# Start and end of a modulated, routed feed-forward kernel: the first demodulation factors worked out for 16 batches alone, both halves of x scaled on VectorE for six groups, one set of positions behind a transposition, and the last block's sums finished one after the other

## The chip, the cores and the metric

The kernel runs on one core of a Trainium2 chip. The metric is the device time of one execution in microseconds (us); lower is better. A core has five engines with an instruction queue each: TensorE (PE in the profile, its weight loads apart as PEld), VectorE (DVE), ScalarE (ACT), GpSimd (POOL) and SyncE (SP). They wait for each other by semaphores.

## The reference

x is 128 batches of 64 tokens with 256 features (8192 tokens). Each batch has a condition vector y. A layer scales and projects the tokens, and a mixture of 8 experts with 2 chosen per token follows; its result is added to x.

```
ys = y * scale
d = rsqrt(einsum('bi,io->bo', ys*ys, weight*weight) + 1e-8)
hidden = einsum('bsi,io->bso', x * ys[:, None, :], weight) * d[:, None, :]
logits = hidden @ wr.T;  vals, idx = top_k(logits, 2)
gating = softmax over the two chosen
pos = cumsum(mask) - 1;  keep = mask & (pos < 2560)      # slot of a token in its expert
h = gelu(xg[e] @ w1[e] + b1[e]);  y = h @ w2[e] + b2[e]  # F = 1024
out = x + segment_sum(y * gate, token)
```

## The kernel before

**The front.** The 8192 tokens are worked on in 16 groups of 512 (8 batches each), four groups to a set. Features lie on partitions, in a lower and an upper half of 128. For each group g: x is scaled by ys (`scale_x`: the lower half in eight ScalarE instructions, one for each batch, L717; the upper half in one of VectorE, L856; for group 0 alone VectorE does the lower half too, L860). TensorE makes the two halves of the product in `modulate(g)` (L501; four matmuls, which the trace shows as eight records; three banks `m_bank` take turns, so half number c waits until half c-3 has been read). `scale_hidden(g)` multiplies them by d (lower half: eight ScalarE instructions, L752; upper half: one of VectorE, L912). `turn_back(g)` on TensorE turns the result back to rows of tokens, four tiles a group, with the router's logits (L514, L516); three banks take turns, so that the fourth tile waits for the copy of the first by ScalarE (`copy_back`, L737). On TensorE group g's `turn_back` stands behind `modulate(g+1)`. x has a ring of four tiles; SyncE loads group g+4 once `modulate(g)` is done.

d comes out of a product of the squares (L485, after 44 warm-up matmuls at L481): VectorE adds epsilon for all 128 batches (`var_t`, 256 columns, L862), ScalarE takes the root (L721), VectorE inverts it (L865) and refines it in four steps (L867 to L873).

For each set, VectorE's `choose` finds the two experts and writes `mask` (L934), TensorE's `positions` counts (L530 to L535), VectorE's `find_slots` and `set_gates` follow, and ScalarE takes one exponential (`odds`, L742). VectorE's `list_group` and TensorE's `list_slots` (L549) make the token lists of each expert. From group 2 on ScalarE also splits a piece of expert 0's weights a group (`split_piece`, L728), and VectorE subtracts (L881). Every engine runs its own list in program order.

**The blocks.** After the front, blocks of up to 384 slots (the last ones of an expert have 256) are gathered, go through `first_product` (L594 to L596), GELU on ScalarE twice (L784), a rounding remainder on VectorE (`split_chunk`, L1169), and `second_product` (L607 to L609, three matmuls for each slice s of 128 slots and each chunk f of eight). At the end of a block VectorE adds a bias (`add_bias`, L1191) and multiplies by the gate (`weigh`, L1197), and GpSimd adds the rows into the output by one indirect DMA for each slice (L425); where a block has two slices, one of 16 spare rows stands ahead of them (L418). In the last block the two slices' sums share one bank, and `y_done` is raised once for both.

## Time and profile before

| | |
|---|---|
| Time, median of 3 runs | 919.29 us (919.23 to 919.46) |
| The profiled execution: its own time, its span | 920.08 us, 918.1 us |
| PE busy, DVE busy, ACT busy, POOL busy | 98%, 53%, 60%, 48% of the span |
| Granted TensorE clock, mean | 0.996 |
| First matmul of group 0 / of block 0 (after the front) | at 8.66 us / at 110.94 us |
| Last matmul ends | near 906.75 us |

Times of the trace are microseconds from the start of the span. The span is what the instructions cover; the execution's own time lies about 2 us over it, and the median of the three unprofiled runs 0.8 us under that.

### The profile page before, as it was taken

To read this page: it belongs to the slowest core of one execution; us is meant where nothing else is said; L and a number is where in the kernel's file an instruction comes from. 1 tells how busy PE (TensorE), PEld (TensorE's weight loads), DVE (VectorE), ACT (ScalarE), POOL (GpSimd) and SP (SyncE) were. 2 spreads that over 40 slices of the span, in tenths; PEclk is the share of its full clock that TensorE was granted. 3 is DMA by queue.
4 is the path that set the end of the run, shared out by engine and by line. 5 is a ranking of instruction groups with operands and counts; after the bars stand their busy time and mean duration, and the time that the engine had idled before them with its cause. 6 is when DMAs were issued, how large, how long until landed. Compare 5 with 4: busy or idle time off the path is not lost.

```text
span 918.1 us, 20295 instructions
## 1 busy us (share of the span) xinstructions
PE 896.6 (98%) x6605; PEld 859.7 (94%) x6605; DVE 484.0 (53%) x1155; ACT 552.1 (60%) x1331; POOL 436.8 (48%) x473
## 2 busy tenths in 40 slices
PE   8999999999999999999999999999999999999995
PEld 5566799999999999999999999999999999999994
DVE  4498877536454554545444554445455544444442
ACT  5988655656556665666556665665566655655552
POOL 0000304645546645665446645655566534664543
PEclk9999999999999999999999999999999999999998
DMA  9676392442523442343523442345234322342232
GB/s 346 208 245 220 105 347 45 67 124 54 132 42 57 66 126 47 54 64 52 134 36 53 69 115 55 59 60 134 42 51 70 47 41 42 50 67 36 47 47 25
DMA packets 56142, 84.47 MB, mean 92 GB/s; under 512 B 6864, under 2 KB 45296, under 8 KB 55696
## 3 DMA queue, kind: packets, MB, share of 16 engines
q0 software_dynamic: 28624, 38.21, 26.9%
q1 hardware_dynamic: 25760, 44.87, 14.5%
q8 instruction: 37, 0.61, 0.3%
q10 hardware_dynamic: 1696, 0.58, 0.2%
q14 instruction: 25, 0.20, 0.1%
HBM read 53.71 MB, written 38.32 MB: 100 GB/s over the span
## 4 chain that ended last, share of the span: by engine, by line
PE 92%; DVE 4%; ACT 2%; issue 1%; DMA 1%; POOLq 0%; ACTq 0%; SPq 0%; DVEq 0%; POOL 0%
PE bank L594 14%; PE bank L607 14%; PE bank L596 14%; PE bank L608 14%; PE bank L609 14%; PE bank L595 14%; PE bank L582 3%; PE bank L501 3%; PE bank L514 1%; PE bank L516 1%; PE bank L549 1%; DMA sb_w<-in_w 1%; DVE sb_w_lo L881 0%; ACT sb_hid_t L752 0%; POOLq L94 0%
## 5 line engine op out<-in xcount | busy, mean ns | idle before, releaser
L784 ACT ACTIVATE sb_h_raw<-bank,sb_b_now 128x384 f32<-128x384 f32 (+1 forms) x416 | 223.6, 538 | 250.1 <-PE bank L596 235.0
L1169 DVE TENSOR_TENSOR sb_h_lo<-sb_h_raw,sb_h_hi 128x384 fp32r<-128x384 f32 (+1 forms) x416 | 213.8, 514 | 264.8 <-ACT sb_h_hi L784 240.3
L607 PE MATMUL bank<-sb_w_hi,sb_h_hi 128*128 128x256 f32 x1064 | 304.4, 286 | 0.0
L608 PE MATMUL bank<-sb_w_lo,sb_h_hi 128*128 128x256 f32 x1064 | 299.8, 282 | 0.0
L425 POOL DMA_INDIRECT out_rows<-sb_y,sb_add_ids x154 | 253.7, 1647 | 95.5 <-issue 55.5
L609 PE MATMUL bank<-sb_w_hi,sb_h_lo 128*128 128x256 f32 x1064 | 298.7, 281 | 0.0
L594 PE MATMUL bank<-sb_xt_hi,sb_w_hi 128*128 128x384 f32 (+1 forms) x832 | 264.1, 317 | 1.5 <-ACT sb_h_hi L784 1.4
L595 PE MATMUL bank<-sb_xt_lo,sb_w_hi 128*128 128x384 f32 (+1 forms) x832 | 260.2, 313 | 0.0
L596 PE MATMUL bank<-sb_xt_hi,sb_w_lo 128*128 128x384 f32 (+1 forms) x832 | 260.2, 313 | 0.0
L784 ACT ACTIVATE sb_h_hi<-bank,sb_b_now 128x384 fp32r<-128x384 f32 (+1 forms) x416 | 221.0, 531 | 0.0
L609 PEld LDWEIGHTS bank<-sb_w_hi,sb_h_lo 128*128 128x128 f32 x1064 | 200.8, 189 | 0.0
L608 PEld LDWEIGHTS bank<-sb_w_lo,sb_h_hi 128*128 128x128 f32 x1064 | 200.4, 188 | 0.0
L607 PEld LDWEIGHTS bank<-sb_w_hi,sb_h_hi 128*128 128x128 f32 x1064 | 200.3, 188 | 0.0
L404 POOL DMA_INDIRECT sb_xg<-hidden,sb_gather_ids x133 | 140.3, 1055 | 70.9 <-POOL sb_ids_ring L400 43.6
L594 PEld LDWEIGHTS bank<-sb_xt_hi,sb_w_hi 128*128 128x128 f32 x832 | 156.4, 188 | 3.0 <-ACT sb_h_hi L784 2.1
L595 PEld LDWEIGHTS bank<-sb_xt_lo,sb_w_hi 128*128 128x128 f32 x832 | 156.6, 188 | 0.0
L596 PEld LDWEIGHTS bank<-sb_xt_hi,sb_w_lo 128*128 128x128 f32 x832 | 156.5, 188 | 0.0
L397 POOL COPY sb_gather_ids<-sb_ids 128x3 int32 (+2 forms) x52 | 10.0, 192 | 300.2 <-DVE sb_gates L1163 172.1
L1154 DVE TENSOR_TENSOR sb_xt_lo<-bank,sb_xt_hi 128x384 fp32r<-128x384 f32 x104 | 53.2, 553 | 74.8 <-ACT sb_xt_hi L759 74.7
L759 ACT CAST sb_xt_hi<-bank 128x384 fp32r<-128x384 f32 x104 | 44.9, 484 | 77.8 <-PE bank L596 75.8
L1191 DVE TENSOR_TENSOR sb_y<-bank,sb_b 128x256 f32<-128x256 f32 x133 | 49.0, 419 | 52.2 <-PE bank L609 49.9
L501 PE MATMUL bank<-sb_x,sb_w 128*128 128x512 f32 x128 | 57.9, 595 | 0.9 <-ACT sb_hid_t L752 0.8
(144 smaller groups left out, 586.1 us busy)
## 6 DMA issues: line engine op xcount, KB each, us to landing
sb_w_raw<-in_w SPq DMA_DIRECT2D x16, 1024.0 KB
hidden<-sb_rows SPq DMA_DIRECT2D x4, 2112.0 KB, 10.0
sb_x<-in_x_t SPq DMA_DIRECT2D x16, 512.0 KB, 5.5
out_rows<-in_x SPq DMA_DIRECT2D x16, 512.0 KB, 7.5
out_rows<-sb_y,sb_add_ids POOLq DMA_INDIRECT x156
sb_xg<-hidden,sb_gather_ids POOLq DMA_INDIRECT x133
sb_b<-in_b SPq DMA_DIRECT2D x1, 1024.0 KB, 10.0
hidden<-sb_empty SPq DMA_DIRECT2D x4, 132.0 KB, 7.9
```

The costliest lines, as they stand in the source:

```text
L404: pool.indirect_dma_start(xg[:, s, :], None, hidden[0:PAD + sets * TS * P, :], bass.IndirectOffsetOnAxis(gather_ids[:, s:s + 1], axis=0),) ...
L425: pool.indirect_dma_start(out, bass.IndirectOffsetOnAxis(add_ids[:, s:s + 1], axis=0), y[s][:, :], None, compute_op=ALU.add,).then_inc(add ...
L501: mm = pe.matmul(m_bank[c % M_RING][:, :], w_sb[:, k, o * P:(o + 1) * P], x_in[g % X_RING][:, k, :], start=(k == 0), stop=(k == KC - 1))
L594: pe.matmul(h, w_hi[u][:, cols], xt_hi[:, rows], start=(k == 0), stop=False)
L595: pe.matmul(h, w_hi[u][:, cols], xt_lo[:, rows], start=False, stop=False)
L596: mm = pe.matmul(h, w_lo[u][:, cols], xt_hi[:, rows], start=False, stop=(k == KC - 1))
L607: pe.matmul(y, hi, w_hi[u][:, cols], start=(f == 0 and s != 1), stop=False, skip_group_check=True)
L608: pe.matmul(y, hi, w_lo[u][:, cols], start=False, stop=False, skip_group_check=True)
L609: mm = pe.matmul(y, lo, w_hi[u][:, cols], start=False, stop=(f == FC - 1), skip_group_check=True)
L784: ins = act.activation(h[:, 0:subs * P], h_bank[f % H_BANKS][:, 0:subs * P], ACT.Gelu_apprx_tanh, bias=b1_now[u][:, f:f + 1])
L1154: dve.tensor_tensor(xt_lo[:, rows_k], x_bank[k][:, 0:SLOTS], xt_hi[:, rows_k].bitcast(F32), ALU.subtract).then_inc(xt_ready, 1)
L1169: dve.tensor_tensor(h_lo[f % RING][:, cols], h_raw[f % RING][:, cols], h_hi[f % RING][:, cols].bitcast(F32), ALU.subtract).then_inc(h_read ...
```

## The change

Six edits. (1) d is worked out in two parts, `D_PARTS`: the 16 batches of groups 0 and 1 (32 columns), then the other 112 (224 columns). (2) VectorE scales the lower half of x too for groups 0 to 5 (`BOTH_HALVES = 6`, `scale_lower`), and ScalarE starts with group 6. (3) For set 0, TensorE's `positions(0)` stands behind `turn_back(4)` instead of ahead of it. (4) ScalarE's `odds` stands behind `copy_back`, for the first three sets. (5) In the last block of the last expert (`last_block`) the last four chunks of slice 0 are all added up ahead of those of slice 1, slice 1 has a bank of its own, the spare rows' DMA is left out, and the last DMAs have a semaphore of their own. (6) 66 warm-up matmuls instead of 44.

```diff
-WARM = 44
+WARM = 66
+BOTH_HALVES = 6
+FIRST_BATCHES = 2 * GB
+        D_PARTS = (slice(0, FIRST_BATCHES), slice(FIRST_BATCHES, B))
 # TensorE
             def modulate(g):
-                if g == 0:
-                    pe.wait_ge(xs_first, 1)
+                if g < BOTH_HALVES:
+                    pe.wait_ge(xs_first, g + 1)
                 else:
-                    pe.wait_ge(xs_lower, g)
+                    pe.wait_ge(xs_lower, g + 1 - BOTH_HALVES)
...
-                if g % JOINED == 1 and g > JOINED:
+                first_set = g == JOINED + 1
+                if g % JOINED == 1 and g > JOINED and not first_set:
                     positions(g // JOINED - 1)
                 turn_back(g - 1)
+                if first_set:
+                    positions(0)
...
+            def last_block(u, b):
...
+                    if f - 3 < FC - RING:
+                        chunk_split(b, f - 3)
+                        for s in range(SHORT):
+                            second_product(u, f - 3, SHORT, only=s)
+                for s in range(SHORT):
+                    for f in range(FC - RING, FC):
+                        chunk_split(b, f)
+                        second_product(u, f, SHORT, only=s)
 # ScalarE
-            act.wait_ge(set_dve, 5)
-            act.activation(root_t[:, :], var_t[:, :], ACT.Sqrt).then_inc(set_act, 1)
-            scale_x(1)
+            for i, part in enumerate(D_PARTS):
+                act.wait_ge(var_ready, i + 1)
+                act.activation(root_t[:, :, part], var_t[:, :, part], ACT.Sqrt).then_inc(set_act, 1)
...
-            act.wait_ge(set_dve, 10)
+            act.wait_ge(d_ready, 1)
             scale_hidden(0)
             for g in range(GROUPS):
-                if g + 2 < GROUPS:
+                if BOTH_HALVES <= g + 2 < GROUPS:
                     scale_x(g + 2)
                 if g + 1 < GROUPS:
                     scale_hidden(g + 1)
-                if g % JOINED == 0 and g > 0:
-                    odds(g // JOINED - 1)
                 if g == GROUPS - 1:
                     split_rows(0)
                 copy_back(g)
+                if g % JOINED == 0 and g > 0:
+                    odds(g // JOINED - 1)
 # VectorE
+            scale_x(0)
+            scale_lower(0)
+            dve.wait_ge(set_pe, 1)
+            for part in D_PARTS:
+                dve.tensor_scalar(var_t[:, :, part], var_bank[:, :, part], EPS, None, ALU.add).then_inc(var_ready, 1)
+            scale_x(1)
+            inverse(0)
+            factors(0)
+            scale_lower(1)
+            inverse(1)
+            scale_hidden(0)
+            factors(1)
...
             for g in range(GROUPS):
-                scale_hidden(g)
+                if g > 0:
+                    scale_hidden(g)
                 if g + 2 < GROUPS:
                     scale_x(g + 2)
+                if g + 2 < BOTH_HALVES:
+                    scale_lower(g + 2)
 # GpSimd
-                if subs < SUBS:
+                if subs < SUBS and not last:
```

On VectorE this is the stretch from the sum of squares to group 1's result, before the change (`sb_var_t`, `sb_root_t` and `sb_tmp_t` are steps of d; `sb_hid_t` is the product times d):

```order
L860 TENSOR_TENSOR sb_x<-sb_x,sb_ys_t 128x512
L862 TENSOR_SCALAR sb_var_t<-bank 128x256
L856 TENSOR_TENSOR sb_x<-sb_x,sb_ys_t 128x512
L865 RECIPROCAL sb_root_t<-sb_root_t 128x256
L867 TENSOR_TENSOR sb_tmp_t<-sb_root_t 128x256
L869 TENSOR_TENSOR sb_tmp_t<-sb_tmp_t,sb_var_t 128x256
L871 TENSOR_SCALAR sb_tmp_t<-sb_tmp_t 128x256
L873 TENSOR_TENSOR sb_d_t<-sb_tmp_t,sb_root_t 128x256
L875 CAST sb_tri<-sb_tri_f 128x128
L912 TENSOR_TENSOR sb_hid_t<-bank,sb_d_t 128x512
```

and after it, from the second half of the scaled x of group 1 on:

```order
L894 TENSOR_TENSOR sb_x<-sb_x,sb_ys_t 128x512
L917 RECIPROCAL sb_root_t<-sb_root_t 128x2x16
L924 TENSOR_TENSOR sb_tmp_t<-sb_root_t 128x2x16
L926 TENSOR_TENSOR sb_tmp_t<-sb_tmp_t,sb_var_t 128x2x16
L928 TENSOR_SCALAR sb_tmp_t<-sb_tmp_t 128x2x16
L930 TENSOR_TENSOR sb_d_t<-sb_tmp_t,sb_root_t 128x2x16
L900 TENSOR_TENSOR sb_x<-sb_x,sb_ys_t 128x512
L917 RECIPROCAL sb_root_t<-sb_root_t 128x2x112
L909 TENSOR_TENSOR sb_hid_t<-bank,sb_d_t 128x512
L924 TENSOR_TENSOR sb_tmp_t<-sb_root_t 128x2x112
```

The factors of 16 batches now come first and the other part's behind the lower half of x (L900), with group 0's upper half of the result between.

On ScalarE this is the stretch around the first set's exponential, before the change (from group 3's weight piece to the scaling of x for group 7):

```order
L728 CAST sb_w_hi<-sb_w_raw 128x512
L717 ACTIVATE sb_x<-sb_x,sb_ys_t 128x64 x8
L752 ACTIVATE sb_hid_t<-bank,sb_d_t 128x64 x8
L742 ACT_TABLE_LOAD
L742 ACTIVATE sb_ratio<-sb_gap 128x16
L737 COPY sb_rows<-bank 128x264 x4
L728 CAST sb_w_hi<-sb_w_raw 128x512
L717 ACTIVATE sb_x<-sb_x,sb_ys_t 128x64 x8
```

and after it:

```order
L766 CAST sb_w_hi<-sb_w_raw 128x512
L755 ACTIVATE sb_x<-sb_x,sb_ys_t 128x64 x8
L791 ACTIVATE sb_hid_t<-bank,sb_d_t 128x64 x8
L775 COPY sb_rows<-bank 128x264 x4
L780 ACT_TABLE_LOAD
L780 ACTIVATE sb_ratio<-sb_gap 128x16
L766 CAST sb_w_hi<-sb_w_raw 128x512
L755 ACTIVATE sb_x<-sb_x,sb_ys_t 128x64 x8
```

The table load and the exponential moved from ahead of the four copies of group 4 to behind them; the first L755 in this piece is the first that ScalarE has at all now.

## Rows read from the trace of the kernel before

**Rows 1.** The page: busy time of each engine, share of the span, instructions.
```profile
PE 896.6 (98%) x6605; PEld 859.7 (94%) x6605; DVE 484.0 (53%) x1155; ACT 552.1 (60%) x1331; POOL 436.8 (48%) x473
```

**Rows 2.** Windows: length, busy us (instructions) of PE, PEld, DVE, ACT, POOL; granted clock, DMA share, GB/s.
```profile
50.00:60.00 10.00, 9.89 (x52) 6.17 (x51) 10.00 (x17) 9.06 (x38) 0.00 (x0) 1.00 1.07 372
```

**Rows 3.** Timeline to 5.4 us, then to 15: start, length, engine, line, count, [idle<-releaser].
```profile
1.43 4.21 PE L481 MATMUL bank<-sb_ones 128*128 128x128 bf16 x38 [1.43 <-DVE sb_ones L838]
...
1.43 4.54 PE L481 MATMUL bank<-sb_ones 128*128 128x128 bf16 x44 [1.43 <-DVE sb_ones L838]
...
7.42 1.16 PE L485 MATMUL bank<-sb_ysq_t,sb_wsq 128*128 128x128 f32 x8 [1.44 <-DVE sb_wsq L850]
...
8.66 5.39 PE L501 MATMUL bank<-sb_x,sb_w 128*128 128x512 f32 x12
...
9.55 1.75 DVE L865 RECIPROCAL sb_root_t<-sb_root_t 128x256 f32<-128x256 f32 x1
...
13.04 1.75 ACT L752 ACTIVATE sb_hid_t<-bank,sb_d_t 128x64 f32<-128x64 f32 x8 [1.63 <-DVE sb_d_t L873]
...
14.84 1.98 PE L501 MATMUL bank<-sb_x,sb_w 128*128 128x512 f32 x4 [0.79 <-ACT sb_hid_t L752]
```

**Rows 4.** Timeline, groups 2 and 3: one scaling of x, TensorE's products.
```profile
17.47 0.68 DVE L856 TENSOR_TENSOR sb_x<-sb_x,sb_ys_t 128x512 f32<-128x512 f32 x1
...
19.21 3.60 PE L501 MATMUL bank<-sb_x,sb_w 128*128 128x512 f32 x8
...
24.49 3.60 PE L501 MATMUL bank<-sb_x,sb_w 128*128 128x512 f32 x8
```

**Rows 5.** Timeline, VectorE, two small instructions of the gates.
```profile
48.07 0.25 DVE L940 RECIPROCAL sb_gate<-sb_gate 128x16 f32<-128x16 f32 x1
...
48.36 0.17 DVE L941 TENSOR_TENSOR sb_gate<-sb_gate,sb_ratio 128x16 f32<-128x16 f32 x1
```

**Rows 6.** Timeline, TensorE and ScalarE, 35 to 50 us (groups 5 to 7).
```profile
35.30 3.60 PE L501 MATMUL bank<-sb_x,sb_w 128*128 128x512 f32 x8
...
35.78 0.62 ACT L728 CAST sb_w_hi<-sb_w_raw 128x512 fp32r<-128x512 f32 x1
...
39.96 1.28 ACT L742 ACT_TABLE_LOAD   x1
...
40.95 0.23 PE L530 MATMUL bank<-sb_mask,sb_tri 128*128 128x128 bf16 x1 [2.04 <-DVE sb_mask L934]
...
41.26 0.22 ACT L742 ACTIVATE sb_ratio<-sb_gap 128x16 f32<-128x16 f32 x1
...
43.48 3.60 PE L501 MATMUL bank<-sb_x,sb_w 128*128 128x512 f32 x8
...
43.96 0.62 ACT L728 CAST sb_w_hi<-sb_w_raw 128x512 fp32r<-128x512 f32 x1
...
47.98 0.97 ACT L737 COPY sb_rows<-bank 128x264 f32<-128x264 f32 x3
...
49.00 3.60 PE L501 MATMUL bank<-sb_x,sb_w 128*128 128x512 f32 x8
...
49.48 0.62 ACT L728 CAST sb_w_hi<-sb_w_raw 128x512 fp32r<-128x512 f32 x1
```

**Rows 7.** Timeline, 903 us to the last instruction.
```profile
903.71 0.28 PE L607 MATMUL bank<-sb_w_hi,sb_h_hi 128*128 128x256 f32 x1
...
904.78 0.42 DVE L1169 TENSOR_TENSOR sb_h_lo<-sb_h_raw,sb_h_hi 128x256 fp32r<-128x256 f32 x1 [1.00 <-ACT sb_h_hi L784]
...
906.79 0.42 DVE L1191 TENSOR_TENSOR sb_y<-bank,sb_b 128x256 f32<-128x256 f32 x1 [1.58 <-PE bank L609]
...
907.43 0.35 DVE L1197 TENSOR_SCALAR sb_y<-sb_y,sb_gates 128x256 f32<-128x256 f32 x1 [0.22 <-DVE sb_y L1191]
...
908.59 1.57 POOL L425 DMA_INDIRECT out_rows<-sb_y,sb_add_ids  x1 [1.13 <-DVE sb_y L1197]
...
910.46 1.55 POOL L425 DMA_INDIRECT out_rows<-sb_y,sb_add_ids  x1 [0.30 <-issue]
```

More of the change, by code:

```diff
@@ L387, in _ @@
             sp.wait_ge(plan_ready, 1)
-            n_all = all_blocks(sp)
-            sp.wait_ge(added, n_all * (16 * SUBS))
+            but_last = all_blocks(sp, less=1) + (LAG - 1)
+            sp.wait_ge(added, but_last * (16 * SUBS))
             sp.sem_inc(sp_paced)
+            sp.wait_ge(added_last, 16 * SHORT)
         @block.gpsimd
@@ L407, in gather, with adds @@
                     ).then_inc(gathered if s < SHORT else gathered_third, 16)
-            def adds(b, subs=SUBS):
+            def adds(b, subs=SUBS, last=False):
                 if not isinstance(b, int) or b > 0:
@@ L427, in adds @@
                         y[s][:, :], None, compute_op=ALU.add,
-                    ).then_inc(added, 16)
+                    ).then_inc(added_last if last else added, 16)
             def next_block(k, tile, sets=SETS, subs=SUBS):
@@ L473, in _ @@
             for i in range(LAG):
-                adds(rest + i, SHORT)
+                adds(rest + i, SHORT, last=(i == LAG - 1))
         @block.tensor
@@ L597, in first_product, with second_product @@
                 mm.then_inc(h_open, 1)
-            def second_product(u, f, subs=SUBS):
+            def second_product(u, f, subs=SUBS, only=None):
                 cols = slice(WCOLS + f * D, WCOLS + (f + 1) * D)
-                for s in range(subs):
+                for s in range(subs) if only is None else (only,):
                     hi = h_hi[f % RING][:, s * P:(s + 1) * P]
                     lo = h_lo[f % RING][:, s * P:(s + 1) * P]
-                    y = y_bank[s]
-                    pe.matmul(y, hi, w_hi[u][:, cols], start=(f == 0 and s != 1), stop=False, skip_group_check=True)
+                    y = y_bank[s] if only is None else last_y_bank[s]
+                    pe.matmul(y, hi, w_hi[u][:, cols], start=(f == 0 and (s != 1 or only is not None)), stop=False,
+                              skip_group_check=True)
                     pe.matmul(y, hi, w_lo[u][:, cols], start=False, stop=False, skip_group_check=True)
                     mm = pe.matmul(y, lo, w_hi[u][:, cols], start=False, stop=(f == FC - 1), skip_group_check=True)
-                    if f == FC - 1 and s > 0:
+                    if f == FC - 1 and only is not None:
+                        mm.then_inc(y_done, 1)
+                    elif f == FC - 1 and s > 0:
                         mm.then_inc(y_done, SUBS - subs + 1)
@@ L655, in one_block @@
                 second_product(u, FC - 1, subs)
+            def last_block(u, b):
+                bank_read(b, 0)
+                first_product(u, 2, SHORT)
+                for f in range(3, FC):
+                    bank_read(b, f - 2)
+                    first_product(u, f, SHORT)
+                    if f == 3:
+                        pe.wait_ge(y_read, b * SUBS + SUBS)
+                    if f - 3 < FC - RING:
[6 more added lines that the diff above has]
+                        second_product(u, f, SHORT, only=s)
             pe.wait_ge(gathered, 16 * SHORT)
@@ L682, in expert @@
                 if e == E - 1:
-                    one_block(u, None, end - 1, so_far, subs=SHORT)
+                    last_block(u, end - 1)
                 else:
@@ L856, in scale_x, with scale_lower, scale_hidden @@
                 dve.tensor_tensor(cols, cols, by_batch(ys_t, 1, g), ALU.mult).then_inc(xs_upper, 1)
+            def scale_lower(g):
+                dve.wait_ge(x_loaded[g % X_RING], 16 * (g // X_RING + 1))
+                cols = x_in[g % X_RING][:, 0, :].rearrange("p (b s) -> p b s", s=S)
+                dve.tensor_tensor(cols, cols, by_batch(ys_t, 0, g), ALU.mult).then_inc(xs_first, 1)
+            def scale_hidden(g):
+                dve.wait_ge(d_ready, 1 if g < 2 else 2)
+                if g >= 2:
+                    dve.wait_ge(back_done, TILES * (g - 1))
+                c = KC * g + 1
+                dve.wait_ge(m_done, c + 1)
+                dve.tensor_tensor(hid_t[g % 2][:, 1, :].rearrange("p (b s) -> p b s", s=S),
+                                  m_bank[c % M_RING][:, :].rearrange("p (b s) -> p b s", s=S),
+                                  by_batch(d_t, 1, g), ALU.mult).then_inc(hid_upper, 1)
@@ new lines, in inverse, with factors @@
+            def inverse(i):
+                part = D_PARTS[i]
+                dve.wait_ge(set_act, i + 1)
+                dve.reciprocal(root_t[:, :, part], root_t[:, :, part]).then_inc(d_step, 1)
+            def factors(i):
+                part = D_PARTS[i]
+                root, tmp = root_t[:, :, part], tmp_t[:, :, part]
+                dve.wait_ge(d_step, 4 * i + 1)
+                dve.tensor_tensor(tmp, root, root, ALU.mult).then_inc(d_step, 1)
+                dve.wait_ge(d_step, 4 * i + 2)
+                dve.tensor_tensor(tmp, tmp, var_t[:, :, part], ALU.mult).then_inc(d_step, 1)
+                dve.wait_ge(d_step, 4 * i + 3)
+                dve.tensor_scalar(tmp, tmp, -0.5, 1.5, ALU.mult, ALU.add).then_inc(d_step, 1)
+                dve.wait_ge(d_step, 4 * i + 4)
+                dve.tensor_tensor(d_t[:, :, part], tmp, root, ALU.mult).then_inc(d_ready, 1)
@@ L1220, in one_block @@
                 for s in range(subs):
-                    add_bias(e, b, s, subs)
+                    add_bias(e, b, s, subs, last)
                     if last:
```

43 lines of the change are left out of this document (14 added, 29 removed).

## The prediction

> **What bounds the kernel now.** The page first: TensorE is busy 98% of the span, no other engine over 60% [rows 1]. So a gain has to come from time in which TensorE stands still, and a loss from a new stand. I looked for its gaps in the timeline, engine by engine. They lie at the two ends: in the front (groups 0 to 15) and behind the last matmul. In the blocks between TensorE runs through, so a shift of the front reaches the end whole. Four stands matter here. Half 3 of the products starts at 14.84, after a stand of 0.79 for ScalarE's scaled result, which itself had waited 1.63 for d until 13.04 [rows 3]. Group 2 starts at 19.21 [rows 4], after a turn in which the fourth tile waited for the first one's copy. `positions(0)` at 40.95 waits 2.04 for the mask [rows 6]. And from the last matmul to the last indirect DMA it is a chain: bias, gate, then GpSimd's two DMAs of 1.57 and 1.55, the second right behind the first [rows 7].
>
> **Warm-up, 22 more matmuls.** 44 take 4.54 us, 0.103 each [rows 3], and end 1.44 before L485, which waits for VectorE. At that mean 22 more cost 2.27 and would end 0.8 late. But the mean hides two paces. The first 38 take 4.21, 0.11 each (128 columns at 1.2 GHz); the last six add 4.54 - 4.21 = 0.33, 0.055 each, the upper level [rows 3]. There 22 cost 1.2, less than the 1.44. I take 0; the other end is +0.8.
>
> **d for 16 batches, and x on VectorE.** Nothing in the trace has 32 columns. A reciprocal takes 0.25 at 16 columns [rows 5] and 1.75 at 256 [rows 3], 6.3 ns a column, so 0.35 at 32 and 1.55 at 224. A product takes 0.17 at 16 [rows 5]; I take 0.19, and 0.04 between dependent ones. The walk on VectorE: epsilon for the first part starts when L485 ends (7.42 + 1.16, so 8.6) and takes 0.2, for the second 0.4, with 0.08 overlap (to 9.1); upper half of x, group 1, 0.68 [rows 4] (to 9.7); reciprocal 0.35 (10.0); four small steps at 0.23 (10.95). ScalarE's `scale_hidden(0)` starts at about 10.97 instead of 13.04 and ends, 1.75 later, at 12.7. TensorE's first 12 records end the pipelined way at 8.66 + 5.39 - 0.16 = 13.9 (0.16 is how far a record reaches over the next start). Half 3 is then held by nothing: 13.9 instead of 14.84.
>
> VectorE pays for it: `scale_lower(1)` ends at 11.5, and TensorE wants it at 12.2 (slack 0.6). Then reciprocal 1.55, `scale_hidden(0)` 0.68 (as wide), four steps near 0.42, the cast 0.2, both halves of x of group 2 at 0.68: 16.95. TensorE's half 3 ends at 13.9 + 1.72 = 15.62, `turn_back(0)` takes 1.85 (5.28 from 19.21 to 24.49 [rows 4], less 3.44 for a group's products), so it wants group 2 at 17.47 (slack 0.5). ScalarE no longer has `scale_x` between, scales group 1 by 15.7 and copies tile by tile, so the fourth tile's stand goes as well. Group 2 starts at 17.47 instead of 19.21: **1.74 us**. For groups 2 to 5 ScalarE loses eight instructions each and VectorE gains one of 0.68; both stay under TensorE's 5.28 a group. The two groups from 24.49 to 35.30 take 10.81 where 2 x 5.28 is 10.56: **0.25 us**. Group 5 starts at 33.32. The loads of x are issued by the same counts, up to 2 us earlier; group 4's is wanted after 23 us and is priced at nothing.
>
> **Positions behind the turn, exponential behind the copies.** ScalarE's weight piece starts 0.48 behind group 5 (35.78 against 35.30), so at 33.80. From there to the mask's use is 5.17 (40.95), so `positions(0)` may start at 38.97; `turn_back(4)` now lies ahead of it and fills the 2.04 stand. From 40.95 to 43.48 is 2.53 with a turn of 1.85 in it: positions cost 0.68, and group 6 starts at 39.65, 3.8 earlier [rows 6]. That isn't kept, for ScalarE is late next. From 33.80 it needs 4.18 to where the table load stands now (39.96): 37.98. Four copies take 1.50 (47.98 to 49.48): 39.48. Table load 1.28 and exponential about 0.22, which used to lie in ScalarE's wait for TensorE, now stand on its path: 40.98. From its weight piece to the start of group 7 it was 43.96 to 49.00, 5.04, and group 7 starts at 46.02 instead of 49.00 [rows 6]. The gain is 2.98, so this part adds 2.98 - 1.99 = **0.99 us**. VectorE waits for the same weight piece and is then busy without a gap (10.00 of 10 us in 50 to 60 [rows 2]), so its lists come earlier by the same 3.0. For set 1 the exponential moves in the same way, without a table load, some 0.22 again [rows 6]: **-0.2 us**. Set 2's lies beside slack: 0.
>
> At that point a page of the Trainium skill speaks against the change. The row has 1.28 for the load, and the exponential starts at 41.26, 0.02 behind it [rows 6]. The Trainium skill, ScalarE: Activation LUTs, What ACT_TABLE_LOAD costs, adds a drain of about 1380 ns to the load's 1283 ns, some 2.66 us for a switch. The trace agrees with the load alone. By the page the sum below would be 1.4 smaller.
>
> **The last block.** Slice 0 has twelve matmuls from 903.71 on, at 0.12 (24 matmuls from 903.71 to 906.79, less one's 0.28, over 23). Nine end at 904.79; the last three need the remainder of chunk 7, ready at 904.78 + 0.42 and 0.06 for the signal, 905.26. So TensorE stands 0.47, and slice 0 is whole at 905.26 + 0.24 + 0.28, read at 905.83 instead of 906.79: 0.96. Slice 1 is whole at 907.22, goes through bias and gate (0.42 + 0.22 + 0.35) and the 0.81 that GpSimd takes to start: 909.07. GpSimd's first DMA starts at 907.63, its second at 910.46 - 0.96 = 909.50, behind the first and not behind slice 1 (slack 0.4). The spare rows' DMA would have ended just there; leaving it out is worth about 0.1 that is in this sum. **0.96 us**.
>
> **Sum.** 1.74 + 0.25 + 0.99 - 0.20 + 0.96 = 3.74. The profiled execution would go from 920.08 to 916.3 (span 914.4); the runs' median lies 0.8 under it, so 919.29 becomes **915.5**. A run of this kernel tells 0.2% (1.8 us) from nothing.
>
> **Rivals.**
> - *The small steps cost as much as the whole ones.* Upper ends: 1.75 and 0.46 a step. Then d comes at 13.3, `scale_lower(1)` at 13.9, TensorE waits 1.7 for group 1, and the first term is gone: 917.3. Against it, 16 columns take 0.25 and 0.17 [rows 5]. 0.05.
> - *The table switch costs 2.66 now that work stands right behind it.* 1.38 less: 916.9. Against it, the exponential runs 0.02 behind the load [rows 6]. 0.05. That is the price of the Trainium skill's page named above.
> - *ScalarE isn't the one that holds group 7* (copies overlap more). TensorE alone would start it at 39.65 + 5.28 = 44.9, gain 4.1: 914.5. 0.06.
> - *The front gives its gain back* between 50 and 100 us, where VectorE has no gap [rows 2]: one more 2 to 3 us in its list before the second mask, as a wait for ScalarE's weight pieces, and only the end's 0.96 stays: 918.3, no change. For it, both engines are nearly full there; against it, nothing is added there but 0.2. 0.08.
> - *Slower: TensorE's clock.* If the longer warm-up is followed by a fall to 1.2 GHz, each L501 record costs 0.43 more. 9 such records eat the forecast, 13 make it slower by over 0.2%; both of groups 0 and 1 (16 records) give +6.9, 922.4. Against it: in the trace the pace rises within the 44, and L501's records are at the upper level behind 1.44 of idleness, which now shrinks to 0.2 [rows 3]. 0.03.
>
> **How the numbers follow.** The forecast has 0.71, with 914.9 to 916.5 of its own (slacks of 0.4 to 0.6 at three places, warm-up +0.8). The range takes in the small steps and ScalarE's rival: 914.5 to 917.3. Faster by over 0.2%: 0.71 + 0.05 + 0.05 + 0.06 and 0.02 for what I didn't think of, 0.89. Within: 0.08. Slower: 0.03.
>
> **What would show it.** Right: half 3 of the products starts near 13.9 without a stand; group 2 at 17.5, group 5 at 33.3, group 7 at 46.0, with a stand in the turn before it; block 0's first matmul near 108.2 (now 110.94); the last two indirect DMAs start 1.87 apart, near 904.9 and 906.7. Wrong: TensorE waiting for `sb_x` in groups 1 to 5, a gap behind the table load, L501 records 0.86 apart, or a second DMA that starts later than 0.3 behind the first.

## The result: slower by 0.8%, and the profile after

The changed kernel takes 927.11 us (median of 6 runs, 926.68 to 930.26), the kernel before 919.46 in the same comparison; the ratio is 1.0082 (95% interval 1.0060 to 1.0103). The forecast was 915.5. The profiled execution of the changed kernel takes 929.16 us, its span is 927.0, 8.9 above before; that is 2.05 above the median of its own runs, so the trace shows somewhat more loss than the medians (7.65). Four executions in all the comparisons (one of the changed kernel with x's halves on VectorE for two groups, three of the kernel before) took 1094 us or more and are left out.

The page of the changed kernel: busy time, the queue that brings code (`q14 instruction`: packets, MB, share), and the chain that ended last. Behind it the same queue's line of the page of before.

```profile
PE 903.6 (97%) x6627; PEld 866.5 (93%) x6627; DVE 486.7 (52%) x1166; ACT 543.0 (59%) x1292; POOL 436.4 (47%) x472
...
q14 instruction: 34, 0.28, 0.1%
...
PE 92%; issue 3%; ACT 2%; DVE 2%; DVEq 0%; ACTq 0%; POOLq 0%; POOL 0%
```

```profile
q14 instruction: 25, 0.20, 0.1%
```

The front went as worked out. The timeline of the changed kernel, TensorE (start, duration, engine, line, operation, idle time before it), beside [rows 3], [rows 4] and [rows 6]:

```profile
7.96 1.11 PE L496 MATMUL bank<-sb_ysq_t,sb_wsq 128*128 128x128 f32 x8
...
17.63 0.59 PE L512 MATMUL bank<-sb_x,sb_w 128*128 128x512 f32 x1
...
33.49 1.02 PE L512 MATMUL bank<-sb_x,sb_w 128*128 128x512 f32 x2
...
46.05 1.02 PE L512 MATMUL bank<-sb_x,sb_w 128*128 128x512 f32 x2
...
108.20 0.42 PE L609 MATMUL bank<-sb_xt_hi,sb_w_hi 128*128 128x384 f32 x1
```

The products run from 8.91 to group 1's end without a stand, so the one at half 3 is gone. Group 2 starts at 17.63 (forecast 17.47), group 5 at 33.49 (33.32), group 7 at 46.05 (46.02; a stand of 0.69 in the turn ahead of it), block 0 at 108.20 (108.2; before 110.94). The end went so too: the last two indirect DMAs start 1.87 apart, and the later one 5.68 behind the last chunk's first GELU (913.80); in the kernel before it is 6.55 (903.91 and 910.46 [rows 7]), so 0.87 are gained, and by the end of the span 0.99.

```profile
913.80 0.47 ACT L823 ACTIVATE sb_h_raw<-bank,sb_b_now 128x256 f32<-128x256 f32 x1 [0.58 <-PE bank L611]
...
917.61 1.57 POOL L436 DMA_INDIRECT out_rows<-sb_y,sb_add_ids  x1 [2.46 <-DVE sb_y L1260]
...
919.48 1.57 POOL L436 DMA_INDIRECT out_rows<-sb_y,sb_add_ids  x1 [0.30 <-issue]
```

**Where the 8.9 us came from.** I laid the starts of all 416 GELU pairs of the two traces side by side. The changed kernel is 2.7 us ahead at block 0, 1.2 ahead some chunks later, 4.3 behind after block 19, 9.9 behind after block 32, and 9.9 at the last one. So there are three steps (in block 0, behind block 19 and behind block 32) and nothing between. The windows around the last two, of before and then of the changed kernel (length, busy us and instructions of PE, PEld, DVE, ACT, POOL, granted clock, DMA share, GB/s):

```profile
400.00:430.00 30.00, 30.00 (x221) 29.96 (x220) 14.78 (x35) 18.53 (x40) 18.16 (x20) 1.00 0.36 60
...
600.00:630.00 30.00, 30.00 (x215) 29.95 (x215) 16.49 (x37) 19.72 (x41) 18.31 (x19) 1.00 0.37 58
```

```profile
400.00:430.00 30.00, 26.60 (x183) 26.03 (x182) 11.53 (x26) 15.87 (x35) 13.56 (x15) 0.94 0.31 47
600.00:630.00 30.00, 26.20 (x183) 25.64 (x182) 11.96 (x28) 16.10 (x35) 14.23 (x14) 0.94 0.33 51
```

TensorE stands 3.4 and 3.8 us (2.9 and 3.4 of it for ScalarE's GELU, 0.5 at most each time for VectorE) and then runs at a lower clock. The changed kernel's windows of 2 us show the fall, and the same fall in block 0, where the stand ahead of it is 1.0 us (110.5 to 111.6), as long as in the kernel before, whose clock there stays at 1.00:

```profile
112.00:114.00 2.00, 1.50 (x25) 1.35 (x22) 1.59 (x6) 1.97 (x6) 0.00 (x0) 0.81 0.93 286
114.00:116.00 2.00, 2.00 (x8) 2.00 (x8) 1.83 (x10) 0.57 (x2) 0.00 (x0) 0.50 0.95 332
116.00:118.00 2.00, 2.00 (x14) 2.00 (x14) 1.86 (x13) 1.45 (x4) 0.00 (x0) 0.84 0.96 350
412.00:414.00 2.00, 1.55 (x8) 1.56 (x9) 1.57 (x4) 1.53 (x4) 0.00 (x0) 0.90 0.26 68
414.00:416.00 2.00, 2.00 (x9) 2.00 (x8) 0.64 (x3) 1.64 (x4) 0.78 (x1) 0.50 0.01 4
416.00:418.00 2.00, 2.00 (x13) 2.00 (x13) 0.00 (x0) 1.28 (x3) 1.70 (x2) 0.75 0.33 26
```

0.50 is the lower of the two levels (1.2 GHz), and a fall costs 0.2 + 1.0 + 0.5 = 1.7 us. So the two places cost 3.4 + 1.7 and 3.8 + 1.7, 10.6 together, block 0's fall 1.7 at most; front and end give 2.7 + 1.0 back. That is 8.6 of the 8.9. Block 0's fall seems to come by chance: below, e13_dve_only has it too, and e4_hint and e15_head_slot, with the same instructions up to there, don't.

What holds TensorE from 409.5 to 412.4 is ScalarE's GELU, and ScalarE itself waits for nothing that the profile shows. ScalarE in the kernel before, and in the changed one, at the same work:

```profile
406.57 0.49 ACT L784 ACTIVATE sb_h_raw<-bank,sb_b_now 128x256 f32<-128x256 f32 x1
406.94 0.49 ACT L784 ACTIVATE sb_h_hi<-bank,sb_b_now 128x256 fp32r<-128x256 f32 x1
407.29 0.21 ACT L798 COPY sb_b_now<-sb_b 128x8 f32 x1
408.31 0.58 ACT L784 ACTIVATE sb_h_raw<-bank,sb_b_now 128x384 f32<-128x384 f32 x1 [0.80 <-PE bank L596]
```

```profile
405.39 0.49 ACT L823 ACTIVATE sb_h_raw<-bank,sb_b_now 128x256 f32<-128x256 f32 x1
405.76 0.49 ACT L823 ACTIVATE sb_h_hi<-bank,sb_b_now 128x256 fp32r<-128x256 f32 x1
408.74 0.20 ACT L837 COPY sb_b_now<-sb_b 128x8 f32 x1 [2.49 <-issue]
411.34 0.58 ACT L823 ACTIVATE sb_h_raw<-bank,sb_b_now 128x384 f32<-128x384 f32 x1 [2.41 <-issue]
```

The copy is the first thing that ScalarE does in each pass of its loop over pairs of experts (`act.Fori(0, E // 2 - 1)`, L816 before, L855 after). In the trace's records of ScalarE's own queue the branch back to the loop's start stands at 405.38, the loop's first instruction follows at 408.61, 3.2 us later (before: 0.27), its 4th, number 449 of the list, at 408.96, and its 5th, number 450, at 410.76, 1.8 us later. At the second way back, from 606.89 on, the two waits are 3.7 and 1.9. The queue that brings code is at work just there: from 400 to 430 us, and again from 600 to 630, it moves 7 packets in the changed kernel and 3 in the one before. Four of the 7 start at 406.2, 406.9, 409.2 and 411.8; the other three, as the 3 of before, follow VectorE's own way back.

**Theory.** The edits took 39 instructions out of ScalarE's list ahead of this loop (40 scalings of x fewer, one root more; the pages have x1331 and x1292), so the loop of 265 instructions starts at number 446 of the list and not at 485. Suppose an instruction memory is filled by blocks, and a border between two blocks lies 4 instructions behind the start, at 450, where the second wait stands. The loop then touches three blocks where it touched two; if two are held, each way back finds its first block gone, and then the next. The Trainium skill, Runtime: NRT & Kernel Launch, Instruction fetch mechanics, has this rule: 512 instructions are held for most engines, refilled 256 at a time, and a taken branch to a block that isn't there stops the engine until it has come. By its figures, as an estimate, a loop of 265 fits if it starts 0 to 247 behind a border and not if it starts 1 to 8 ahead of one. The runs below agree: with 4 and 1 instructions ahead of the border ScalarE waits, with its loop 0, 4, 34 and 35 behind it doesn't. What they test is differences of place; the number 450 itself hangs on how the list is counted. **Rivals:** the stand comes from when the branch falls or what other traffic there is; or from some other part of the change.

### The profile page after: what moved, and what is told of

The parts are those of the page before. It is cut to its first block, busy times and chain, and to the rows that moved or that the text cites. A ratio compares the mean times of both kernels' runs of the same rounds, so it can differ in the third digit from the quotient of the medians.

```text
span 927.0 us, 20314 instructions
## 1 busy us (share of the span) xinstructions
PE 903.6 (97%) x6627; PEld 866.5 (93%) x6627; DVE 486.7 (52%) x1166; ACT 543.0 (59%) x1292; POOL 436.4 (47%) x472
## 4 chain that ended last, share of the span: by engine, by line
PE 92%; issue 3%; ACT 2%; DVE 2%; DVEq 0%; ACTq 0%; POOLq 0%; POOL 0%
PE bank L609 13%; PE bank L623 13%; PE bank L625 13%; PE bank L626 13%; PE bank L610 13%; PE bank L611 13%; PE bank L512 5%; PE bank L597 3%; PE bank L525 2%; PE bank L527 1%; PE bank L560 1%; PE bank L492 1%; ACT sb_x L755 0%; ACT sb_h_hi L823 0%; ACT sb_hid_t L791 0%
```

## The experiments

In all but e4_hint and e15_head_slot the place of a loop is moved by instructions that do nothing (`sem_inc` on a semaphore that nobody waits for), 7 behind each chunk in the first blocks. "S" and "V" are the numbers in the list at which ScalarE's and VectorE's loop over pairs starts. Ratios are to the kernel before, run beside them on the same chip; times of different rounds are from different chips, and the kernel before itself had medians from 919.5 to 921.1, so differences of a few tenths of a us between rows say little.

| run | S | V | us (median) | ratio (95%) |
|---|---|---|---|---|
| kernel before | 485 | 435 | 919.5 to 921.1 | 1 |
| changed kernel | 446 | 448 | 927.11 | 1.0082 (1.0060 to 1.0103) |
| e1_pad39 | 485 | 448 | 919.69 | 0.9987 (0.9977 to 0.9996) |
| e2_before217 (before) | 702 | 435 | 929.46 | 1.0099 (1.0080 to 1.0118) |
| e3_pad8 | 454 | 448 | 920.73 | 0.9998 (0.9988 to 1.0007) |
| e4_hint | moved, see below | 448 | 920.88 | 0.9993 (0.9982 to 1.0004) |
| e5_both_lists | 485 | 464 | 916.08 | 0.9948 (0.9935 to 0.9961) |
| e6_before_dve (before) | 485 | 464 | 921.57 | 0.9999 (0.9988 to 1.0010) |
| e7_warm44 | 485 | 464 | 916.48 | 0.9952 (0.9939 to 0.9965) |
| e8_no_last | 485 | 464 | 917.10 | 0.9965 (0.9952 to 0.9979) |
| e9_border3 | 449 | 464 | 922.93 | 1.0031 (1.0016 to 1.0046) |
| e10_border4 | 450 | 464 | 915.94 | 0.9954 (0.9941 to 0.9968) |
| e11_old_order | 485 | 464 | 916.93 | 0.9959 (0.9947 to 0.9971) |
| e12_two_groups | 484 | 464 | 916.10 | 0.9953 (0.9939 to 0.9968) |
| e13_dve_only | 446 | 464 | 926.03 | 1.0062 (1.0046 to 1.0077) |
| e14_whole_d | 485 | 464 | 918.77 | 0.9975 (0.9965 to 0.9985) |
| e15_head_slot | placed | placed | 915.56 | 0.9945 (0.9931 to 0.9959) |

### Is it the place of ScalarE's loop?

```diff
+            pads = [39]            # 217 in e2, 8 in e3
             def gelu(u, b, f, subs=SUBS):
...
                 ins.then_inc(gelu_done, 1)
+                for _ in range(min(7, pads[0])):
+                    act.sem_inc(padded)
+                    pads[0] -= 1
```

> The changed kernel with 39 empty ScalarE instructions (semaphore increments that nobody waits for, 7 behind each chunk's activation in its first blocks), so that its loop over pairs of experts starts at instruction 485 of ScalarE's list, as it does before the change, and not at 446. Nothing that is computed differs. Theory (the loop of 265 instructions touches three blocks of the instruction memory where it starts, and each way back to its start waits for code): both stands of TensorE behind ScalarE at the way back (2.89 and 3.42 us) go, with the clock's fall behind them, some 5.2 us each; what is left is what stood ahead of the first way back (1.28 us ahead of before) and the tail (0.99): 919.46 - 2.27 = 917.2 us, 916.8 to 917.6. Rival A (the stand comes from where the branch falls in time, or from other work of the change, not from the list's layout): 927.1 us, as the changed kernel. Rival B (the pads themselves delay the activations): above 918, with stands of TensorE in the first four blocks.

> The kernel before, with 217 empty ScalarE instructions of the same kind (7 behind each chunk's activation, over its first four blocks), so that its loop over pairs starts at instruction 702 = 446 + 256, at the same place in a block of 256 as in the changed kernel. Nothing of the change is in it. Theory (layout alone): two ways back of the loop with 3.2 and 1.8 us in which ScalarE waits for nothing shown, a stand of TensorE of about 3 us at each and the clock's fall behind it: 919.46 + 10.8 = 930.3 us, 929 to 931.5. Rival A (not the layout): 919.5 us, or up to 920.5 if the pads cost something.

> The changed kernel with 8 empty ScalarE instructions, so that the loop starts at 454. In the trace the second wait of a way back stands between the loop's 4th and 5th instruction, so a block's border should lie 4 behind the start; 8 pads put the start behind the border and the loop of 265 into two blocks. Theory: 917.2 us, 916.8 to 917.6, as with 39 pads. Rival C (what counts is how long the list is, by degrees, or the border is elsewhere): 927.1 us, or something between.

The kernel before, with nothing but empty instructions added, gets slower by 1.0% (929.46; expected 929 to 931.5), with two stands of 2.9 to 3.1 us at the same two ways back, and in the profiled execution a clock fall behind the first. ScalarE's waits there are 3.0 and 3.2 us behind the branch and 2.0 and 2.1 between the 4th and 5th instruction: 702 is 446 + 256, and the waits come at the same places of the loop, which is what shows the 256. The changed kernel loses its loss with 39, and with 8. So the place of the loop is the cause, and neither the change's work nor its timing is needed for it. But both times missed the 917.2 by 2.5 and 3.5 us. The waits of TensorE in e1_pad39 say why:

```profile
PE bank L624 <- DVE sb_h_lo L1238: 3.1, 3, 1.4
```

and VectorE in the same trace:

```profile
408.80 0.65 DVE L1266 TENSOR_SCALAR sb_y<-sb_y,sb_gates 128x256 f32<-128x256 f32 x2
414.74 0.56 DVE L1238 TENSOR_TENSOR sb_h_lo<-sb_h_raw,sb_h_hi 128x384 fp32r<-128x384 f32 x1 [5.29 <-issue]
```

VectorE has such a loop as well, of 362 instructions. Its queue's records show 2.8 to 3.1 us behind the branch in both kernels. Before the change that is all, and TensorE doesn't notice: the loop starts at 435 and lies across the border of 450 too, but 15 instructions behind its start, and no wait shows there. After it (13 instructions more ahead of the loop) the step from its 2nd to its 3rd instruction, at 450 in its list too, takes 2.2 to 2.8 us where it takes 0.35 before, and in e1_pad39 TensorE stands 1.4 us at each way back.

### A hint in place of the move

```diff
-            with act.Fori(0, E // 2 - 1) as pair:
+            with nc.Fori(0, E // 2 - 1, engines=..., hint_back_edge=True) as pair:
```

> The changed kernel with a prefetch hint for the branch back at the head of ScalarE's loop over pairs (one more instruction in the loop, the list otherwise as in the change). Theory: if the hint fetches the loop's first block ahead of the branch, the first wait (3.2 us) goes, and the second (1.8 us), for the block behind the border, may stay and is hidden: waits of 5.0 us made a stand of 2.89, so some 2.1 us are covered. Then 917 to 919 us. If the hint does nothing, 927.1 us; if it throws out a block that is still wanted, above 927.

ScalarE's waits are gone, both of them, and the time is that of e3_pad8. It is over the 917 to 919 that were expected, for at the ways back VectorE holds TensorE, 2.9 us at the longest (1.9 in e3_pad8; the second line below is of two short stands elsewhere, 0.5 and 0.9 us, which every run with ScalarE's loop out of the way has, and the kernel before too). But the loop was not left where it was. A step over a border shows in the first pass too: in the changed kernel the loop's 5th instruction starts 0.38 us behind the 4th (203.02 and 203.40), in e10_border4 below, whose loop starts on the border, the first one starts 0.37 behind the instruction ahead of it (200.08 and 200.45), and elsewhere such steps take 0.06 to 0.08. In e4_hint the step between the same 4th and 5th takes 0.08, and the long one, 0.51, stands ahead of the loop's first instruction (200.04 and 200.55). So by the trace the loop starts on a border with this edit, which is enough to free it (e10_border4), and the run doesn't show what the hint itself does.

```profile
PE bank L624 <- DVE sb_h_lo L1233: 5.0, 3, 2.9
PE bank L610 <- ACT sb_h_hi L824: 1.4, 2, 0.9
```

### Both loops clear of the border

The same empty instructions in VectorE's `split_chunk`: 16 in the changed kernel, 29 in the kernel before.

> The changed kernel with 39 empty instructions in ScalarE's list and 16 in VectorE's (semaphore increments that nobody waits for, in the first blocks), so that ScalarE's loop over pairs starts at 485 and VectorE's at 464. Background: with ScalarE's loop moved, the trace shows VectorE next: at the way back of its own loop (362 instructions, from 448 in the change, 435 before) it waits 2.92 us behind the branch and, other than before the change, 1.92 us more between the loop's 2nd and 3rd instruction, and TensorE stands 1.38 and 1.43 us behind it. 450, where that second wait lies, is the place of ScalarE's second wait too. Theory (at 464 the loop's 362 instructions lie in two blocks): both waits go, at both ways back, and the two stands, 1.65 and 1.71 us by the chunk times: 0.9987 - 3.36/920 = 0.995 of before, 0.9942 to 0.9960, some 915.6 us where before takes 919.5. Rival A (only the second wait goes, or VectorE's code waits are moved elsewhere): 0.9965 to 0.9987. Rival B (the stand has another cause): 0.9987, as with ScalarE's loop alone.

> The kernel before, with 29 empty instructions in VectorE's list alone, so that its loop over pairs starts at 464 and not 435; ScalarE's starts at 485 as it is. So both loops lie as in the changed kernel with both lists padded, and the ratio of the two is that of the change by itself. In the kernel before VectorE waits 2.88 us at each way back, and TensorE doesn't stand. Theory (those waits were covered): they go from the trace and the time stays, 0.9995 to 1.0010 of before. Rival (they held something up after all): down to 0.997.

0.9948 where 0.995 was expected; 916.08 us is 0.6 above the forecast of the change. With its loops in the same places the kernel before doesn't move (0.9999): its one covered wait was worth nothing. So some 0.5% is what the change is worth by itself, and 0.35% (3.2 us) against the runs of the kernel before that have no clock fall in them, near 919.3.

### Where the border is, to one instruction

VectorE's 16 stay; ScalarE's pads are 3, 4 and none.

> The changed kernel with 16 empty instructions in VectorE's list, as in the run with both lists padded, and only 3 in ScalarE's: its loop over pairs starts at 449, one ahead of the border that the traces put at 450. Theory (three blocks are touched as soon as one instruction of the loop lies ahead of the border): ScalarE waits twice at each way back, TensorE stands some 3 us and its clock falls: 10.4 us more than with both lists padded, some 926.5 us, 1.0045 to 1.0075 of before. Rival (the border is not there, or what counts is how much lies ahead of it): 0.9935 to 0.9965, or between.

> The same with 4 empty instructions in ScalarE's list: its loop starts at 450, on the border. One empty instruction more than in the run beside it. Theory: 916 us, 0.9935 to 0.9965 of before, as with both lists padded. Rival (the border is a few instructions off): near the run with 3, 1.0045 to 1.0075.

> The changed kernel with 16 empty instructions in VectorE's list alone (loop at 464), ScalarE's loop left at 446. Together with the changed kernel and the run with 3 and 16 it tells what VectorE's code waits add beside ScalarE's. Background: with ScalarE's loop at 449 and VectorE's at 464, ScalarE waited 2.6 and 2.0 us, TensorE stood 2.3 at the first way back, and the kernel took 922.9; the changed kernel has 3.2 and 1.8, stands of 2.9 and 3.4, and 927.1. Theory A (the two engines' code is fetched at the same time and each makes the other's longer, and a longer stand brings the clock's fall more often): 921.5 to 924, as with 3 and 16. Theory B (the difference is in how much of ScalarE's loop lies ahead of the border, 4 instructions and not 1): 926 to 928.

One empty instruction, 3 to 4, takes 7.0 us off. ScalarE with 3 and with 4:

```profile
404.04 0.49 ACT L827 ACTIVATE sb_h_hi<-bank,sb_b_now 128x256 fp32r<-128x256 f32 x1
408.18 0.20 ACT L844 COPY sb_b_now<-sb_b 128x8 f32 x1 [3.66 <-issue]
409.08 0.58 ACT L827 ACTIVATE sb_h_raw<-bank,sb_b_now 128x384 f32<-128x384 f32 x1 [0.69 <-ACT sb_b_now L844]
```

```profile
404.25 0.49 ACT L827 ACTIVATE sb_h_hi<-bank,sb_b_now 128x256 fp32r<-128x256 f32 x1
404.61 0.22 ACT L844 COPY sb_b_now<-sb_b 128x8 f32 x1
```

With 3, both waits lie ahead of the copy (2.6 us to the first instruction, 2.1 to the second), for now only that first one is ahead of the border; in the changed kernel four were, and the second wait lay behind the copy. That is the border of 450 by a second sign. A third is the queue that brings code: from 400 to 430 us it moves 3 packets in e9_border3 and none in e10_border4. The windows of the run with 3:

```profile
400.00:430.00 30.00, 27.68 (x190) 27.43 (x189) 12.71 (x28) 16.05 (x34) 14.67 (x17) 0.94 0.30 46
600.00:630.00 30.00, 27.73 (x199) 27.48 (x198) 14.28 (x33) 16.79 (x37) 16.51 (x18) 1.00 0.34 55
```

The stands are 2.3 each here, and the clock falls behind one of them only; 926.5 was expected and 922.93 came. With ScalarE's loop at 446 (e13) they are 3.2 and 2.8, again with one fall behind them in the profiled execution and a second one in block 0, and the time is 926.03, where theory B had 926 to 928. The stands bear B out, the time less so: of the 3.2 us between the two profiled executions 1.7 is block 0's fall. Most of the changed kernel's loss doesn't need VectorE's waits. How the length of the waits hangs on how many instructions lie ahead of the border was seen (3.0 to 3.7 us behind the branch and four packets of code with four, 2.5 to 2.7 and three packets with one), not explained.

### The change's own parts, with both loops out of the way

```diff
 # e7_warm44
-WARM = 66
+WARM = 44
 # e8_no_last
-                    last_block(u, end - 1)
+                    one_block(u, None, end - 1, so_far, subs=SHORT)
...
-                    add_bias(e, b, s, subs, last)
+                    add_bias(e, b, s, subs)
 # e11_old_order: `positions` ahead of `turn_back` for every set, `odds` ahead of `copy_back`
 # e12_two_groups
-BOTH_HALVES = 6
+BOTH_HALVES = 2
 # e14_whole_d
-        D_PARTS = (slice(0, FIRST_BATCHES), slice(FIRST_BATCHES, B))
+        D_PARTS = (slice(0, B),)
...
-            inverse(1)
             scale_hidden(0)
-            factors(1)
```

> The changed kernel with both lists padded (39 and 16) and the warm-up back at 44 matmuls for 66. In the changed kernel's trace group 0's first matmul starts at 7.96 us, before it at 7.42. Theory (the long warm-up holds group 0 up by 0.5 us and gives nothing back): 0.3 to 0.6 us less than with both lists padded alone. Rival A (group 0 is held by its data or by the clock's level, not by the warm-up): within 0.2 us. Rival B (with the short warm-up TensorE stands between it and group 0 and the clock rises later): 0.5 us or more slower.

The median is 0.4 us over e5_both_lists, and not the 0.3 to 0.6 under it that was expected. But the six runs fall into three of 915.3 to 915.9 and three of 917.0 to 917.6, where e5_both_lists has all five within 915.5 to 916.1. The profiled execution is one of the slower three, and shows what the 22 matmuls do: with 44 the eight matmuls behind the warm-up take 2.08, at the lower clock level, and group 2 starts at 18.60; with 66 they take 1.16, and it starts at 17.68. That the faster three had the clock up in time wasn't seen, for they have no profile.

```profile
1.43 4.87 PE L494 MATMUL bank<-sb_ones 128*128 128x128 bf16 x44 [1.43 <-DVE sb_ones L884]
7.25 2.08 PE L498 MATMUL bank<-sb_ysq_t,sb_wsq 128*128 128x128 f32 x8 [0.95 <-DVE sb_wsq L895]
```

```profile
1.43 5.61 PE L494 MATMUL bank<-sb_ones 128*128 128x128 bf16 x66 [1.43 <-DVE sb_ones L884]
7.64 1.16 PE L498 MATMUL bank<-sb_ysq_t,sb_wsq 128*128 128x128 f32 x8 [0.59 <-DVE sb_wsq L895]
```

> The changed kernel with both lists padded (39 and 16), and the last block's products back in the old order on TensorE and VectorE (both row slices' sums in turn, one sign for both); GpSimd's part for the last block stays as changed. Theory (term of 0.96 us in the sum; the stretch from the last activation to the end fell from 14.2 to 13.2 us): 0.8 to 1.0 us more than with both lists padded alone. Rival (most of it comes from GpSimd's last adds, which don't wait for the spare row's): 0.4 us or less.

1.0 us more. From the last chunk's first GELU to the last indirect DMA it is 6.55 us, as in the kernel before, and 5.70 in e5_both_lists, so 0.85 of it is there. The last block's sums carry the term of 0.96, and GpSimd's part nothing that shows.

> The changed kernel with both lists padded (39 and 16) and the first set's positions ahead of the turn back again on TensorE, ScalarE's odds ahead of the copies again. The sum put the two moves at 0.99 us. Theory: 0.8 to 1.2 us more than with both lists padded, with a stand of about 2 us at the first set's positions in place of 0.7 at the turn back. Rival A (the set's chain on VectorE, not the order on TensorE, sets it): 0.3 us or less. Rival B (the lists further on depend on it too): over 1.5.

916.93 against 916.08 and 915.94: 0.85 to 1.0 more, with TensorE's stand of 2.0 at the positions back. The run takes the later sets' exponentials back as well, so what it should cost by the sum is 0.99 - 0.20 = 0.79. It is near enough to bear the term out.

> The changed kernel with VectorE scaling both halves of x for 2 groups and not 6, so that ScalarE scales the lower half from group 2 on, as before; loops at 484 (ScalarE, 6 empty instructions) and 464 (VectorE, 20). d of the first 16 batches is still worked out early. The sum put the early d and the halves together at 1.74 us, most of it the stand of 0.79 at half 3 and 0.42 at group 2 and what follows. Theory (ScalarE's time in the first groups was the limit, so the halves carry the gain behind group 1): 0.6 to 1.4 us more than with both lists padded. Rival A (the early d alone does it): within 0.3 us. Rival B (VectorE has too much with six groups, and two are better): up to 0.5 us less.

916.10, no difference. VectorE's scaling of the lower half for groups 2 to 5 is worth nothing here; rival A holds.

> The changed kernel with d worked out for all 128 batches at once, as before, and everything else as changed; loops at 485 and 464 as with both lists padded. The run with x's halves on VectorE for two groups gave no difference, so the first term (1.74 us) should hang on the early d alone. Theory: d comes some 2 us later, half 3 stands again, VectorE's scaling of group 1's halves comes after the whole d: 1.2 to 2.2 us more than with both lists padded, 0.9965 to 0.9975 of before. Rival (the halves and the early d each do it alone; with no scaling of group 1 ahead of it ScalarE catches up by group 2): within 0.4 us.

918.77, 2.7 us more in the median and 1.4 in the profiled execution (span 915.4 against 914.0), and TensorE waits for group 1's lower half:

```profile
13.53 0.70 PE L514 MATMUL bank<-sb_x,sb_w 128*128 128x512 f32 x1 [1.32 <-DVE sb_x L907]
```

So the first term hangs on the early d, as long as VectorE scales group 1's lower half too; the old d with that half on ScalarE was not tried. Group 2 starts at 18.92 (17.68 in e5_both_lists), so 1.24 us are d's; the twelve runs fall into five of 917.0 to 917.7 at a mean clock of 0.996 or 0.997 and seven of 918.8 to 919.3 at 0.994 or 0.995, so the median has a clock fall in it, and 0.9 to 1.6 us is what d costs without one.

### The best version

The changed kernel without empty instructions, each of the two loops' heads placed at 16 of a block (`head_slot`).

> The changed kernel without empty instructions; instead each of the two loops over pairs (ScalarE's and VectorE's) has its first instruction placed at place 16 of a block of 256 by an alignment of the loop's head. Theory: the same as both lists padded, 915.5 to 916.5 us, 0.9935 to 0.9965 of before, plus at most one code wait at the loop's entry that stands once. Rival (the place that is asked for isn't where the loop is loaded, or the entry's jump costs a stand of about 3 us and a clock fall): 918 to 921.

915.56 us, 0.9945 of before (0.9931 to 0.9959), level with e5_both_lists and e10_border4, and the number that was forecast for the change. That the two agree to 0.1 us is in part luck: the forecast was for the kernel without placed loops, and the kernel before, that it started from, moves by more than that from run to run. The windows from 400 to 430 and from 600 to 630 have TensorE busy for 30.00 of 30.00 at a clock of 1.00, and the queue that brings code moves nothing in them:

```profile
400.00:430.00 30.00, 30.00 (x218) 29.96 (x217) 16.78 (x37) 19.17 (x40) 18.06 (x20) 1.00 0.35 54
600.00:630.00 30.00, 30.00 (x214) 29.93 (x212) 17.43 (x37) 19.89 (x41) 18.02 (x19) 1.00 0.36 55
```

## Why the prediction was wrong

- **"In the blocks between TensorE runs through, so a shift of the front reaches the end whole."** This step failed. The first half is true of the kernel before; the second doesn't follow from it. It took it that instructions that the diff doesn't touch take the same time. The front's shift did reach block 0 whole (2.74 of 2.78 us), and behind it the blocks gave it back and more: ScalarE, at two ways back of its loop, waited for code, TensorE stood 3.4 and 3.8 us, and its clock fell each time (1.7). Those instructions stand in a list, and the diff changed how many stand ahead of them. The rows that could have warned are not durations but numbers: ScalarE's list 39 shorter, a loop of 265 instructions that is run again, and two ways back. It cost 10.6 us by the traces (11.0 between the medians of the changed kernel and of e5_both_lists), near three times the sum. VectorE's loop had the same fault, worth 3.6 us once ScalarE's was out of the way (919.69 and 916.08).
- **The rival on the slower side** (TensorE's clock after a longer warm-up) had the wrong place: the products of groups 0 and 1 ran at the upper level (0.43 a record). The clock fell behind the stands and once in block 0. The case that decided was not among the rivals, and 0.02 for what I didn't think of was too little.
- **The terms of the sum** were near where one was tried: 1.74 for the early d and the halves (1.24 to 1.4 in the traces with the early d taken back; the halves of groups 2 to 5 brought nothing), 0.79 for the moves (0.85 to 1.0), 0.96 for the last block (0.85 to 1.0). The 0.25 was not tried by itself; groups 2 to 5 did start 5.28 to 5.29 apart. Together they gave 0.9948 and 0.9945 of before where 3.74 of 919.29 is 0.9959. The kernel before has runs with a clock fall in its front (last heading) that the changed kernel with both lists padded had not, which would account for ratios below the sum's; against the undisturbed 919.3 the 915.94 to 916.08 are 3.2 to 3.4 less, a little under the 3.74. "A run of this kernel tells 0.2% from nothing" was too sure for the same reason: the kernel before's own runs go from 919.0 to 923.3, with mean clocks of 0.996 to 0.990.
- **Warm-up at 0, other end +0.8.** In the changed kernel's profiled execution the next matmuls start 0.5 later: its 66 take 6.69 us, and those start at 7.96 instead of 7.42. Group 0 starts 0.25 later (8.91 for 8.66) and group 2 0.16 later than forecast. In e5_both_lists the 66 take 5.61 and end before VectorE's squares are ready. When the pace rises within them differs from run to run.
- **The table switch.** I took the row's 1.28. In the changed kernel the load stands at 39.61 for 1.28 and the exponential at 40.91, 0.02 behind it, with group 7 on time at 46.05. That rival falls. The 2.66 of the Trainium skill, ScalarE: Activation LUTs, What ACT_TABLE_LOAD costs, is not seen here: its 1283 ns for the load agree, its drain of 1380 doesn't show, and the trace decides.

## What to carry to other kernels

Before an edit is priced, count the instructions of each engine's list up to every loop that is run more than once, and the loop's own: if it is longer than one block of 256, its place decides whether it fits the two that are held, and any edit ahead of it may move it over a border. The 256 and the two are the figures of the page of the Trainium skill named above; e2_before217 agrees with the 256, and a loop of 265 that waits in three blocks and not in two agrees with the two. What shows it in a profile is an engine that waits for "issue" at the first instructions of a loop, and more packets in the queue that brings code (34 and 36 with both loops across a border, 24 or 25 with one, 14 to 16 with none). A loop that is placed on purpose cost nothing here (915.56 us) and makes the comparison of two versions fair; without that, a good change measured 0.8% slower, and empty instructions alone made a kernel 1.0% slower.

## What the runs showed of the hardware that wasn't expected

- A stand of TensorE of some 2 us can be followed by a fall of its clock that costs 1.7 us more, and not every time. Windows of e11_old_order, behind its stand of 2.05 at 38.97:

```profile
38.00:40.00 2.00, 1.03 (x18) 1.03 (x19) 1.69 (x5) 1.47 (x2) 0.00 (x0) 0.82 1.13 315
40.00:42.00 2.00, 2.00 (x10) 2.00 (x10) 0.45 (x1) 0.46 (x2) 0.00 (x0) 0.50 0.50 210
42.00:44.00 2.00, 2.00 (x11) 1.52 (x11) 0.00 (x0) 1.37 (x4) 0.00 (x0) 0.83 0.03 8
```

  The profiled execution of before has the same stand [rows 6] at a clock of 1.00; those of e2_before217 and e6_before_dve, which have it too, show 0.50 from 42 to 44. Five of e11's six runs are 916.7 to 917.0 with a mean clock of 0.996 or 0.997, and the profiled one 918.5 at 0.995. So a part of what the change is worth may lie in falls that no longer come; that was not tried by itself.
- From a way back to the loop's first instruction it is 2.5 to 3.7 us on ScalarE and 2.8 to 3.3 on VectorE where its code is gone, and 0.2 to 0.35 where it is held; the step over the next border right behind it takes 1.7 to 2.2 on ScalarE and 2.2 to 2.8 on VectorE, where it takes 0.1 and 0.35 otherwise.
- Asking for a hint for the branch moved the loop onto a border by itself (e4_hint), so an edit of that kind is a change of place as well, and its time alone doesn't say which of the two helped.
